# Expert rows scaled as they leave PSUM and added in memory, against two stored rows per token and a weighted sum later

## The reference, cut to what matters

```python
probs = softmax(hs @ router_gate.T)
topk_scores, topk_idx = top_k(probs, 2)
topk_scores = topk_scores / sum(topk_scores)
# rows sorted by expert; per row of token t and expert e:
h = (x @ expert_gate_up[e])[1::2] * silu((x @ expert_gate_up[e])[0::2])
out_rows = h @ expert_down[e]
out = zeros_like(hs).at[token_slots].add(out_rows * scores_sorted[:, None])
```

## Time and profile before

| | |
|---|---|
| median of 3 runs | 1266.95 us (1263.74 to 1269.08) |
| profiled execution | 1262.27 us, its span 1260.1 us |
| mean granted TensorE clock | 0.915 |
| PE busy | 1037.3 us, 82% of the span |
| DVE, ACT, POOL busy | 732.1, 474.9, 389.2 us |
| DMA | 261.58 MB, mean 208 GB/s; HBM read 168.59 MB, written 91.82 MB |
| POOL's own queue (gathers and puts) | 13760 packets, 45.10 MB, 10.2% of 16 engines' span |

### The profile page before, as it was taken

How to read it: one execution, slowest core, us unless ns; L and a number is a source line. 1 busy time by engine, 2 the same in 40 slices (tenths; PEclk the granted TensorE clock), 3 DMA queues, 4 the chain that set the end, 5 groups by cost and what they waited for, 6 DMA issues and landing times. The chain is left out here.

```text
span 1260.1 us, 17861 instructions
## 1 busy us (share of the span) xinstructions
PE 1037.3 (82%) x5852; PEld 868.3 (69%) x5852; DVE 732.1 (58%) x1378; ACT 474.9 (38%) x987; POOL 389.2 (31%) x302
## 2 busy tenths in 40 slices
PE   6825798779879988789847998899779998999964
PEld 4513687669877788779846676668658786887742
DVE  5777667977556568676574433765375343443225
ACT  3351136423223244324503435634443443443332
POOL 1144136424531214212103333632233433334210
PEclk9976788899989998899978999999899998999985
DMA  9317248666785476664732247535562787986249
GB/s 286 133 39 248 72 144 285 216 204 224 258 273 194 160 269 214 250 244 184 264 154 67 105 166 284 189 133 185 217 241 79 266 302 282 343 308 237 89 163 329
DMA packets 96356, 261.58 MB, mean 208 GB/s; under 512 B 9944, under 2 KB 50872, under 8 KB 80400
## 3 DMA queue, kind: packets, MB, share of 16 engines
q1 hardware_dynamic: 54680, 147.44, 32.7%
q10 hardware_dynamic: 27832, 67.91, 16.0%
q0 software_dynamic: 13760, 45.10, 10.2%
HBM read 168.59 MB, written 91.82 MB: 207 GB/s over the span
## 5 line engine op out<-in xcount | busy, mean ns | idle before, releaser
L571 POOL TENSOR_TENSOR sb_ring<-sb_raw,sb_ring 128x1024 fp32r<-128x1024 f32 x48 | 126.9, 2651 | 246.7 <-ACT sb_ring L1122 246.7
L627 PE MATMUL ps<-sb_xnH,sb_ring 128*128 128x288 f32 x512 | 168.0, 328 | 37.1 <-DMA sb_ring<-w_dram 16.9
L911 PE MATMUL ps<-sb_w,sb_xtH 128*128 x344 | 154.2, 448 | 22.6 <-DVE sb_hh L1725 12.7
L594 POOL DMA_INDIRECT y_dram<-sb_ysb,sb_target x86 | 87.4, 1016 | 250.1 <-ACT sb_ysb L1212 241.2
L628 PE MATMUL ps<-sb_xnH,sb_ring 128*128 128x288 f32 x512 | 158.2, 309 | 0.0
L629 PE MATMUL ps<-sb_xnL,sb_ring 128*128 128x288 f32 x512 | 158.0, 309 | 0.0
L1718 DVE TENSOR_TENSOR sb_xtL<-ps,sb_xtH 128x512 fp32r<-128x512 f32 x86 | 59.4, 691 | 141.1 <-ACT sb_xtH L1192 141.0
L913 PE MATMUL ps<-sb_w,sb_xtH 128*128 x344 | 139.0, 404 | 0.0
L912 PE MATMUL ps<-sb_w,sb_xtL 128*128 x344 | 138.5, 403 | 0.0
L627 PEld LDWEIGHTS ps<-sb_xnH,sb_ring 128*128 128x128 f32 x512 | 103.4, 202 | 43.9 <-DMA sb_ring<-w_dram 18.5
L585 POOL DMA_INDIRECT sb_xs<-xn_dram,sb_source x86 | 87.7, 1019 | 64.1 <-DVE sb_source L1637 39.2
(11 more groups left out here) (221 smaller groups left out, 2295.7 us busy)
## 6 DMA issues: line engine op xcount, KB each, us to landing
w_dram<-sb_ring SPq DMA_DIRECT2D x48, 1024.0 KB, 6.7
sb_w<-w_dram SPq DMA_DIRECT2D x48, 1024.0 KB, 9.4
sb_ring<-w_dram ACTq DMA_DIRECT2D x24, 1024.0 KB, 6.6
sb_raw<-in_w_ffn SPq DMA_DIRECT2D x24, 512.0 KB, 4.4
sb_raw<-in_w_ffn SPq DMA_DIRECT2D x48, 256.0 KB, 4.5
sb_X<-in_x SPq DMA_DIRECT2D x16, 576.0 KB, 8.8
xn_dram<-sb_XN ACTq DMA_DIRECT2D x18, 512.0 KB, 3.3
sb_g<-y_dram ACTq DMA_DIRECT2D x18, 512.0 KB, 7.1
```

Of the source, the lines that this page charges most:

```text
L571: pool.tensor_tensor(to[:, 1, :], raw[:, r % 2, :], to[:, 0, :].bitcast(f32), ALU.subtract)\
L594: pool.indirect_dma_start(y_dram[h], bass.IndirectOffsetOnAxis(ap=target[:, h, m:m + 1], axis=0), ysb[:, r, :], None).then_inc(y_stored[r] ...
L627: pe.matmul(out_ap, w[0], xh, start=start, stop=False)
L911: pe.matmul(PS[:, 1, :], xtH[:, i % 2, k, :], wh, start=k == 0, stop=False)
```

## The change

Expert rows are scaled before they leave the core. The two scores of a token, as first score and difference (second minus first), are stored behind its normalised row in `xn_dram`, whose rows become 514 numbers; the gather brings them along. A new ACT instruction of one column per tile forms each row's weight (`weight_of` = difference times `pick` plus first score; `pick` says whether the row is the second choice), and `y_copy` scales with it. `put` becomes an adding scatter (`compute_op=ALU.add`) into a table of one row per token and 128 spare rows. It waits, besides the copy, until the put before it has landed. Both tables (2432 rows x 2 KB) are zeroed near the start by two SP transfers that read one zeroed row of the weight ring's last place; the first use of that place waits for them. The combine loads one row per token (256 KB, `gsum`, ring of 8), and PE transposes it straight from there: the ACT scaling and the DVE weighted sum are gone.

```diff
-GRING = 4
+GRING = 8
-    xn_dram = [nc.dram_tensor(f"xn_dram_{h}", (HALF, CH), f32, kind="Internal").ap() for h in range(2)]
-    y_dram = [nc.dram_tensor(f"y_dram_{h}", (2 * HALF + NMC * P, CH), f32, kind="Internal").ap() for h in range(2)]
+    xn_dram = [nc.dram_tensor(f"xn_dram_{h}", (HALF, CH + 2), f32, kind="Internal").ap() for h in range(2)]
+    y_dram = [nc.dram_tensor(f"y_dram_{h}", (HALF + P, CH), f32, kind="Internal").ap() for h in range(2)]
...
@@ place_free
+            elif i == RING - 1:
+                eng.wait_ge(zeroed, 32)
@@ SP, after the images and the first raw pieces
+            sp.wait_ge(zeros, 1)
+            for h in range(2):
+                if h:
+                    sp.wait_ge(bc_in, 16)
+                else:
+                    sp.wait_ge(x_loaded[XG - 1], 16 * (B // XG))
+                sp.dma_start(y_dram[h].rearrange("(p t) c -> p t c", p=P),
+                             ring[:, RING - 1:RING, 0, 0:CH].bitcast(f32).broadcast_to((P, TL + 1, CH)))\
+                    .then_inc(zeroed, 16)
@@ SP, the last combine's loads
             for t in range(TL):
                 n = TL + t
-                if t >= GRING:
-                    sp.wait_ge(gt_ready, n - GRING + 1)
-                else:
-                    sp.wait_ge(gt_ready, TL)
-                sp.dma_start(g12[:, n % GRING, :, :], y_by_tile[t]).then_inc(g_loaded[n % GRING], 16)
+                sp.wait_ge(f_ready, max(n - GRING + 1, TL))
+                sp.dma_start(gsum[:, n % GRING, :], y_by_tile[t]).then_inc(g_loaded[n % GRING], 16)
@@ POOL, gather
+                    pool.wait_ge(scores_out, 16 * (h + 1))
...
                 if i >= XSR:
-                    pool.wait_ge(t_ready, i - XSR + 1)
+                    pool.wait_ge(weight_ready, i - XSR + 1)
@@ POOL, put
                 if m == 0:
                     pool.wait_ge(target_ready, h + 1)
+                    pool.wait_ge(zeroed, 32)
+                if i:
+                    pool.wait_ge(y_stored[1 - r], 16 * ((i + 1) // 2))
                 pool.wait_ge(y_out, i + 1)
                 pool.indirect_dma_start(y_dram[h], bass.IndirectOffsetOnAxis(ap=target[:, h, m:m + 1], axis=0),
-                                        ysb[:, r, :], None).then_inc(y_stored[r], 16)
+                                        ysb[:, r, :], None, compute_op=ALU.add).then_inc(y_stored[r], 16)
@@ PE, combine
-                    pe.wait_ge(gt_ready, n + 1)
+                    pe.wait_ge(g_loaded[n % GRING], 16 * (n // GRING + 1))
@@ ACT, router and x_hi
                 yield step(74)
+                act.wait_ge(scores, h + 1)
+                act.dma_start(xn_dram[h][:, CH:CH + 2].rearrange("(t p) c -> p t c", p=P), score[:, h, :, :])\
+                    .then_inc(scores_out, 16)
...
+                if i % NM == 0:
+                    act.wait_ge(target_ready, i // NM + 1)
+                if i >= 4:
+                    act.wait_ge(y_out, i - 3)
+                act.activation(weight_of[:, i % 4:i % 4 + 1], xs[:, i % XSR, CH + 1:CH + 2], ACT.Identity,
+                               scale=pick[:, i // NM, i % NM:i % NM + 1], bias=xs[:, i % XSR, CH:CH + 1])\
+                    .then_inc(weight_ready, 1)
@@ ACT, y_copy and combine
+                act.wait_ge(weight_ready, i + 1)
-                act.activation(ysb[:, i % 2, :], PS[:, 3, :], ACT.Copy).then_inc(y_out, 1)
+                act.activation(ysb[:, i % 2, :], PS[:, 3, :], ACT.Copy, scale=weight_of[:, i % 4:i % 4 + 1]).then_inc(y_out, 1)
...
-                    act.wait_ge(g_loaded[n % GRING], 16 * (n // GRING + 1))
-                    if n >= 2:
-                        act.wait_ge(gt_ready, n - 1)
-                    act.activation(gs[:, n % 2, :], g12[:, n % GRING, 0, :], ACT.Copy, scale=score[:, h, 0, t:t + 1])\
-                        .then_inc(gs_ready, 1)
@@ DVE, start and combine
+            v.memset(ring[:, RING - 1, 0, 0:CH].bitcast(f32), 0.0).then_inc(zeros, 1)
...
-                        v.scalar_tensor_tensor(gt[:, n % 2, :], g12[:, n % GRING, 1, :], score[:, h, 1, t:t + 1],
-                                               gs[:, n % 2, :], ALU.mult, ALU.add).then_inc(gt_ready, 1)
```

More of the change, by code:

```diff
@@ L168, in metaformer @@
         pVE, pMV, pST6, pRS = sb("pVE", [P, TL]), sb("pMV", [P, TL, 2]), sb("pST6", [P, 2, PG, 6]), sb("pRS", [P, TL])
-        score = sb("score", [P, 2, 2, TL])
+        score = sb("score", [P, 2, TL, 2])
+        pick = sb("pick", [P, 2, NMC])
+        weight_of = sb("weight_of", [P, 4])
         source = sb("source", [P, 2, NMC], i32)
@@ L214, in metaformer @@
         comb = ExitStack()
[L215 to L217 removed]
+        gsum = sb("gsum", [P, GRING, CH], f32, comb)
         comb.close()
@@ L345, in metaformer @@
         g_loaded = ring_of("g_loaded", GRING)
-        gs_ready, gt_ready = sem("gs_ready"), sem("gt_ready")
+        zeros, zeroed, scores, scores_out, weight_ready = (
+            sem("zeros"), sem("zeroed"), sem("scores"), sem("scores_out"), sem("weight_ready"))
         f_ready, f_added, stored = sem("f_ready"), sem("f_added"), sem("stored")
@@ L944, in combine @@
                     for k in range(KC):
-                        last = pe.transpose(PS[:, 4 + n % 4, k * P:(k + 1) * P], gt[:, n % 2, k * P:(k + 1) * P], ident)
+                        last = pe.transpose(PS[:, 4 + n % 4, k * P:(k + 1) * P], gsum[:, n % GRING, k * P:(k + 1) * P], ident)
                     last.then_inc(f_ready, 1)
@@ L1227, in combine @@
                         act.wait_ge(y_stored[r], y_stores(0, r))
-                    for t in range(GRING - 1):
+                    for t in range(GRING - 2):
                         load_rows(t)
@@ L1576, in mixer @@
                 link(v.reciprocal(Q["den"], Q["den"]))
-                link(v.tensor_tensor(score[:, h, 0, :], Q["m1"], Q["den"], ALU.mult))
-                link(v.tensor_tensor(score[:, h, 1, :], Q["m2"], Q["den"], ALU.mult))
+                link(v.tensor_tensor(score[:, h, :, 0], Q["m1"], Q["den"], ALU.mult))
+                link(v.tensor_tensor(score[:, h, :, 1], Q["m2"], Q["den"], ALU.mult))
+                v.tensor_tensor(score[:, h, :, 1], score[:, h, :, 1], score[:, h, :, 0], ALU.subtract).then_inc(scores, 1)
                 yield step(74)
@@ L1628, in mixer @@
                 link(v.tensor_copy(tile_expert[:, h, :], F["expert"]))
-                link(v.tensor_scalar(spare0[:, :], number[:, 0:1], float(2 * HALF - 1), None, ALU.add))
-                link(v.tensor_scalar(F["spare"], iM, float(P), spare0[:, 0:1], ALU.mult, ALU.add))
+                link(v.tensor_scalar(spare0[:, :], number[:, 0:1], float(HALF - 1), None, ALU.add))
                 yield step(82)
@@ L1637, in mixer @@
                 v.tensor_copy(source[:, h, :], F["row"]).then_inc(source_ready, 1)
-                link(v.tensor_scalar(F["second"], PS[:, 7, 0:NMC], 0.0, float(HALF), ALU.not_equal, ALU.mult))
-                link(v.tensor_tensor(F["at"], F["row"], F["second"], ALU.add))
-                link(v.tensor_tensor(F["at"], F["at"], F["spare"], ALU.subtract))
+                link(v.tensor_scalar(pick[:, h, :], PS[:, 7, 0:NMC], 0.0, None, ALU.not_equal))
+                link(v.tensor_scalar(F["at"], F["row"], spare0[:, 0:1], None, ALU.subtract))
                 link(v.tensor_tensor(F["at"], F["at"], F["above"], ALU.mult))
-                link(v.tensor_tensor(F["at"], F["at"], F["spare"], ALU.add))
+                link(v.tensor_scalar(F["at"], F["at"], spare0[:, 0:1], None, ALU.add))
                 v.tensor_copy(target[:, h, :], F["at"]).then_inc(target_ready, 1)
@@ L1732, in combine @@
             def combine(h, at):
-                for t in range(TL + 2):
-                    yield at + 4 * t + 3
+                for t in range(TL):
+                    yield at + 4 * t + 11
                     n = h * TL + t
-                    if t < TL:
-                        v.wait_ge(gs_ready, n + 1)
-                        if n >= 2:
-                            v.wait_ge(f_ready, n - 1)
-                        v.scalar_tensor_tensor(gt[:, n % 2, :], g12[:, n % GRING, 1, :], score[:, h, 1, t:t + 1],
-                                               gs[:, n % 2, :], ALU.mult, ALU.add).then_inc(gt_ready, 1)
-                    if t >= 2:
-                        v.wait_ge(f_ready, n - 1)
-                        dst = X[:, :, tile_of(h, t - 2)]
-                        v.tensor_tensor(dst, dst, PS[:, 4 + (n - 2) % 4, :].rearrange("p (k n) -> p k n", n=P),
-                                        ALU.add).then_inc(f_added, 1)
+                    v.wait_ge(f_ready, n + 1)
+                    dst = X[:, :, tile_of(h, t)]
+                    v.tensor_tensor(dst, dst, PS[:, 4 + n % 4, :].rearrange("p (k n) -> p k n", n=P),
+                                    ALU.add).then_inc(f_added, 1)
             mix = [[Beside(part) for part in (patch(1, 1, SIDE), mixer(1, 1, SIDE + 29, dense))], [Beside(combine(0, 3 * SIDE))]]
```

23 lines of the change are left out of this document (9 added, 14 removed).

## The result

The changed kernel takes **1316.47 us** (median of 4 runs, 1313.06 to 1317.87), the kernel before 1267.99 beside it (4 runs): a ratio of 1.0385 (95% interval 1.0353 to 1.0417). The profiled executions are 1313.06 and 1262.27, 50.8 us apart. The forecast was 1280 with a range of 1251 to 1335: slower, as expected, but +48.5 us (of the medians) instead of +13.5.

What follows compares the result with a forecast made beforehand. PE was taken to bind beside the first combine, transfers in the last. Terms -12 -3 +18 +1 +3 +5 +0.5 +1 = +13.5 gave 1275.8 profiled, 1280 against the median; range 1251 to 1335.

Steps and rivals of the forecast that it cites:

- beside h=0: Puts beside the first half: POOL's product for the scan comes 1.5 us later, twice or so; cost 3 us.
- other h=1 tiles: Tiles at 957 to 1000 and 1140 to 1213, one weight load each: delay absorbed but for 1 us.
- beside the first combine: Waiting puts there: five weight cycles at +4.6 us, less about one tile absorbed by two buffers; cost 18 us.
- the end: Last puts of h=1: 4.4 us apart, the last landing at 1221.1 instead of 1216.0; cost 5 us.
- the first item on the puts: Each put's add lengthens its landing by 1.4 us: unloaded landing 4.2, cycle 4.4, hidden under the 4.82 us pace.
- The weight cycle beside the combine: Five tiles per weight load: 1.5 puts in 14 us, the rest 4.8 each; 30.8 us instead of 26.2, +4.6.
- The rival of two passes: Every put's add is a full read then a full write, unloaded cycle 6.2: +90 us, 1357; chance 0.15.
- Tail: Last put's landing to the end: half the load bytes, transfers still bind; 32 us instead of 44.1, gain 12.
- Start of the first combine: ACT's 4.35 us wait for a load of combine rows goes; gain 3 us.
- Zeroing: Two 5.0 MB transfers near the start, done before the ring's third place is needed: 0, at most 3 us.
- The buffers absorb it: Puts beside the first combine: add costs 0.6 us or less, so their 18 becomes 0 to 3; 1258 us; chance 0.30.
- No change in sum: Whole kernel: the puts' cost, between 8 and 14 us, just pays for the tail; 1263 to 1272 us; chance 0.14.

Runs made afterwards that it cites:

- version 3: Changed kernel with plain puts and no wait between puts; odd tiles go to separate tables and are left out of the output: 1256.70 us, ratio 0.9933.
- versions 7: Version 3 (plain puts, no wait) with rows of `xn_dram` 2304 bytes apart instead of 2056: 1248.05 us, ratio 0.9855.
- 11: Changed kernel, whole computation kept, puts waiting only at expert changes and empty tiles, rows 2304 bytes apart: 1275.18 us, ratio 1.0062.
- versions 2: Changed kernel with adding puts but no wait; odd tiles add into separate tables, left out of the output: 1266.69 us, ratio 1.0008.
- 8: Changed kernel with adding puts, no waits, three tables (one read), three staging buffers, rows 2304 bytes apart: 1262.29 us, ratio 0.9965.
- 12: Version 11 (waits only at expert changes and empty tiles, rows 2304 bytes apart) with a third staging buffer: 1267.84 us, ratio 1.0007.
- version 5: Changed kernel with waiting, adding puts of half the bytes into a table of their own; expert part left out: 1277.16 us, ratio 1.0087.
- version 6: Changed kernel without add, a second plain 32 KB put behind each put, all one at a time: 1388.44 us, ratio 1.0950.

## Why the prediction was right in direction and wrong in size

The working was that the end gains and the puts cost more. The end gained 14.5 (44.1 to 29.6). What the puts cost is the start of the changed kernel's puts less that of version 3 (neither add nor wait), in us:

| | forecast | measured | from the starts of |
|---|---|---|---|
| beside h=0 | 3 | 6 | put 38: 980.7 - 974.9 |
| other h=1 tiles | 1 | 15 | puts 38 to 45: 43.8 - 33.7; puts 71 to 84: 73.3 - 67.9 |
| beside the first combine | 18 | 31 | puts 45 to 71: 168.9 - 137.6 |
| the end | 5 | 7 | puts 84 to 86: 9.9 - 5.4, and a landing 2.2 longer |

Put 1 starts at 694.2 in both. Puts 45 and 71 start at 997.6 and 1140.2 in the kernel before, the ends of the stretch that the forecast took for the combine. Together it is 59 us. Less 14.5, and with the 6.2 by which version 3's last put stands behind that of the kernel before (1219.5 and 1213.3: row pitch and chance), it makes the 51.0 between the two spans.

**The step that failed** is the first item on the puts, the price of the add: "+1.4", hence "Unloaded a put then lands in 4.2, cycle 4.4, under the 4.82 pace: hidden, with 0.4 to spare". A landing takes 4.65 to 4.87, about +2.1, and the cycle 4.98. The bounds, 0 and +3.3, held it; the value chosen lay 0.7 under. That small miss crossed the tile's pace, and with it the sign of what happens between two weight loads. For the tiles outside the combine the sum let puts follow 4.4 us apart and had a load "absorbed but for" 1; they were 4.9 or more apart, fell behind by a further 0.2 to 0.3 a tile instead of catching up, and 15 us were lost. From put 44 to 86, 42 steps took 260.2 us, 6.20 each, for 215.3 or 5.13 in version 3.

**The weight cycle beside the combine**, the second term, was mis-sized as well: 30.8 us for five tiles. From the landing in one load to that in the next (1096.30 to 1129.87 in the chain) five tiles took 33.6, with 10.55 us for the first (its landing and 0.27) and 5.3 to 6.2 for each of the rest. The loaded landing, taken as 9.4, was 10 to 12; the rest were taken as 4.8 and none was. The rival of two passes had cycles of 12.8 and 6.2 and +90; the truth lies between, at 10.3 to 12.1 and 5.0.

**Terms that came out.** The mechanism is as forecast: POOL waits for the put before, ACT for a buffer, PE for ACT (31.8 us on L944). Tail: 29.6 us for 32 forecast. Start of the first combine: version 3 stands 12.0 us behind the kernel before at put 50 (1034.9 and 1022.9) and 6.7 at put 56 (1068.8 and 1062.1), so 5 came back, for 3; no experiment isolates it. Zeroing 0: the ring's third place is copied at 107.84, for 108.59 before. Score store 0: from the scores to the gather's indices 27.1 us (640.9 to 668.0), as before (634.6 to 661.7).

**A term that was missing.** With rows of 2056 bytes the stores of normalised rows landed after 4.5 us instead of 3.3, and ACT waited 33.7 us for them instead of 24.1: 3 to 9 us by the medians of versions 7 and 11. I had named the pitch for gathers alone, with the Trainium skill, "DMA: Bandwidth & Descriptors" (How a descriptor splits into AXI transactions). A piece that starts off a 256-byte boundary is split into more transactions there; the store's landing agrees in direction, and it was the store that was waited for.

**The rivals.** "The buffers absorb it" needed an add of 0.6 or less: measured 2.1. Its rule from the Trainium skill, "DMA: Bandwidth & Descriptors" (Anatomy of one DMA), 2.0 us plus bytes over 436 GB/s, made an estimated 3.2 of an add; the trace does not agree: it shows 4.65 to 4.87. POOL's instruction is 0.6 us longer; whether that and the 64 more packets a put make up the difference was not tried. "Two passes" put an add at +3.3, too dear by 1.2, and the total at 1357. "No change in sum" is where versions 2, 8 and 12 stand (ratios 1.0008, 0.9965, 1.0007): take away the wait or most of it, and the gain at the end about pays for the add.

## What to carry to other kernels

A wait of each transfer for the one before turns a latency into a rate: compare landing plus issue with the pace of the work, not with the buffers. Here, below the pace (landing 2.7 against 4.82) delays were made up and the wait cost 0.6 us; 3% above it (4.98) every delay stayed, and a third buffer gave 5 of 50 us. So price the operation at its margin to that pace, and where the margin is smaller than the uncertainty (here 0.4 us against bounds 3.3 apart), forecast both sides of the threshold, not the middle. And wait only where two transfers can touch the same row: that alone gave back 39 of 49 us.

## What the runs showed of the hardware beside that

- An adding indirect put of 256 KB holds POOL for 1.62 us, a plain one for 0.99; with half the columns it is 1.62 too (139.3 us for 86 in version 5), and the packets are 19264 again. So neither goes with the bytes; the rows, 128 in both, were not varied.
- Landings, unloaded: plain 256 KB 2.7 us, adding 256 KB 4.65 to 4.87, adding 128 KB 3.76, plain 32 KB 2.15 (the second puts of version 6).
- In a weight load an adding put of 256 KB landed after 7.8 to 11.9 us, one of 128 KB after 8.8 to 10.1: half the bytes save little there.
- A store of 512 KB in rows 2056 bytes apart lands after 4.5 us in the median of 18, 2048 apart after 3.3.
